# A routed feed-forward kernel: gathers four units ahead, the last units alone on TensorE, and an opening that turns two small inputs first

## The chip, the cores and the metric

The kernel runs on one core of a Trainium2 chip. The metric is the device time of one execution in microseconds. A core has five engines with instruction streams of their own: TensorE (PE: matrix products and transpositions), VectorE (DVE), ScalarE (ACT), GpSimd (POOL) and SyncE (SP, which here only issues transfers). They wait for each other through semaphores. Each of them takes its instructions in order, so that one that waits holds up all behind it.

## The reference

Two sequences of 2048 rows of 128 channels go through one layer:

```
mod = silu(c) @ wmod                                  # six rows of 128 for each sequence: sa ca ga sb cb gb
h = layernorm(x) * (1 + ca) + sa
x = x + ga * (mean of h over all rows up to this one) # softmax of a causal mask of zeros
h = layernorm(x) * (1 + cb) + sb
scores = softmax(h @ gate.T)                          # 8 experts
the 8192 largest of all 4096 * 8 scores are kept      # gate = score where kept, else 0
out = sum over experts of gate * (gelu(h @ W1 + b1) @ W2 + b2)  +  shared feed-forward of h
x = x + gb * out
```

## The kernel before

**The opening.** The 4096 rows are eight batches of 512. For each batch, DVE takes statistics (`stats1`), POOL makes the scale and bias of the normalisation (`rstd1`), ACT and DVE normalise into `XN` (`norm1`), PE transposes (`turn_x`), DVE forms the running means by a scan (`prefix`, with `INV` = 1 - 1/(t+1) made on ACT by `ratio(q)`), PE adds the transposed-back means to x in PSUM (`add_x`, `add_means`, with the diagonals `DCA`), and DVE adds a constant row `CBR` and keeps x (`keep_x2`). Then follow the second statistics (`stats2`) and normalisation, the logits and the rows written to a scratch tensor in memory. What the two sequences' vectors need comes from `modulation`: silu(c) on ACT, six products with `WMOD` on PE, and a chain of small instructions on DVE. Small vectors (biases, c, gate weights, 1/(t+1)) are loaded as rows of a tile `ROWS` in seven transfers from ACT's queue and transposed together into `COL`.

**The choice.** Thirty steps of a binary search on DVE and PE find the 8192nd score, between the products of the shared feed-forward on PE. Then lists of chosen rows are made (`IDXB`).

**The units.** The chosen pairs are sorted by expert and cut into units of 512 rows; a branch skips units that aren't used (up to 23; this input uses 18, numbered 0 to 17). For a unit v:

- POOL gathers its rows by four indirect transfers (`gather(v, s)`), 128 rows each, into one of ten places of `XG`;
- PE transposes them (`xt(v)`) and ACT copies them to `XT` (`copy_x(v)`);
- PE multiplies with W1 in four steps (`up`), ACT applies gelu to each, PE multiplies with W2 in four steps (`down`), ACT adds the bias (`ye(v)`, tile `YE`);
- PE transposes back (`yt(v)`), DVE multiplies with the scores (`yo(v)`, tile `YO`), which waits until the scatter of unit v - 2 has landed;
- POOL scatters with addition (`scatter(v)`, four indirect transfers), which waits until the scatter of unit v - 1 has landed.

POOL's order is 36 gathers, then for each unit its scatter and behind it a gap in which `gathered(v) - gathered(v - 1)` further gathers are issued. PE, ACT and DVE go through steps `s`, each with a unit v and a part c, four to a unit. `down` follows `up` by `LAG` = 2 steps, so that a unit's last two `down` lie in the next unit's steps. At c = 2 of unit v, PE does `yt(v - 1)` and then `xt(v + 1)`.

The lines of the view names: L920 is a gather, L933 a scatter, L956 a transposition by TensorE, L1067 `up` of a unit, L1093 `down`, L414 gelu, L430 `copy_x`, L439 `ye`, L799 the products of `yo`, L331 `ratio`, L395 `CBR`, L521 `keep_x2`, L997 `add_means`, L978 the products with `WMOD`, L974 the transposition of `ROWS`.

Of the kernel before, what the change touches and what calls it, by code (L numbers as in the profile page):

```python
# [15 lines left out]
P = 128  # L16
# [30 lines left out]
NSTEP = UNIT1 + NC * (NU + 3)  # L47
# [15 lines left out]
def gathered(v):  # L63

    return min(max(NT * AHEAD + PER_GAP * (v + 1), NT * (v + 5)), NT * NU)
# [18 lines left out]

def on_step(s):

    if 0 <= s < GS0:
        return s
    if UNIT1 <= s < UNIT1 + NC * NU:
        return s - UNIT1 + GS0  # L90
    return None


def adaln_moe(nc, x, gw, w1, b1, w2, b2, ws1, bs1, ws2, bs2, c_in, wmod, consts, ucon, icon, inv, out):
    rows_dram = nc.dram_tensor("rows_scratch", [S + NPAD, ROW], F32, kind="Internal").ap()

    with ExitStack() as ctx:
# [135 lines left out]
        def sync(eng):  # L233
# [25 lines left out]
            for b in range(2, NB):  # L259
                load_x(b)  # L260
            for q in range(1, NT):
                eng.dma_start(INV[:, q, :],
                              inv[0, q * BLK:(q + 1) * BLK].partition_broadcast(P)).then_inc(M["ld_inv"], 16)
# [21 lines left out]
            for s in range(NSTEP):  # L285
# [11 lines left out]
                v, c = (s - UNIT1) // NC, (s - UNIT1) % NC  # L297
# [971 lines left out]
```

## Time and profile before

| | us |
|---|---|
| median of 3 runs | 350.27 (349.93 to 351.46) |
| profiled execution, its own time | 349.06 |
| span of that execution | 347.3 |
| PE busy | 274.7 (79%) |
| POOL busy | 213.7 (62%) |
| DVE busy | 152.7 (44%) |
| ACT busy | 139.4 (40%) |

The span is from the first to the last instruction of the profiled execution; its time has some 1.8 us around it. Busy shares are averages over stages with different limits. The start times in the timeline are from the span's start. In a row of the timeline, the square bracket is the idle time before the instruction and what ended it.

### The profile page before, as it was taken

To read this page: it belongs to the slowest core of one execution; us is meant where nothing else is said; L and a number is where in the kernel's file an instruction comes from. 1 tells how busy PE (TensorE), PEld (TensorE's weight loads), DVE (VectorE), ACT (ScalarE), POOL (GpSimd) and SP (SyncE) were. 2 spreads that over 40 slices of the span, in tenths; PEclk is the share of its full clock that TensorE was granted. 3 is DMA by queue.
4 is the path that set the end of the run, shared out by engine and by line. 5 is a ranking of instruction groups with operands and counts; after the bars stand their busy time and mean duration, and the time that the engine had idled before them with its cause. 6 is when DMAs were issued, how large, how long until landed. Compare 5 with 4: busy or idle time off the path is not lost.

```text
span 347.3 us, 4624 instructions
## 1 busy us (share of the span) xinstructions
PE 274.7 (79%) x1044; PEld 141.8 (41%) x1044; DVE 152.7 (44%) x765; ACT 139.4 (40%) x236; POOL 213.7 (62%) x240
## 2 busy tenths in 40 slices
PE   5889985999989999999989899899595697495000
PEld 1757754343445554443444444444243243232000
DVE  2899773567677777344454544422101202102000
ACT  1669874354434434334334434344232333241000
POOL 4657540000027777677888888888787888765670
PEclk9999986899999999999999999999988989988555
DMA  7928420121025976655555665565535634333330
GB/s 205 307 70 227 108 63 0 30 64 15 0 75 143 282 226 174 176 96 84 116 115 114 106 109 114 116 120 119 114 41 127 142 46 68 75 28 33 33 29 1
DMA packets 49774, 35.70 MB, mean 103 GB/s; under 512 B 7816, under 2 KB 44495, under 8 KB 49744
## 3 DMA queue, kind: packets, MB, share of 16 engines
q0 software_dynamic: 13824, 14.46, 25.0%
q1 hardware_dynamic: 35794, 20.86, 21.6%
q8 instruction: 11, 0.18, 0.2%
q14 instruction: 19, 0.16, 0.1%
q10 hardware_dynamic: 126, 0.04, 0.0%
HBM read 23.40 MB, written 11.94 MB: 102 GB/s over the span
## 4 chain that ended last, share of the span: by engine, by line
PE 36%; POOL 17%; issue 14%; DVE 12%; DMA 8%; ACT 4%; SPq 3%; DVEq 1%; POOLq 0%; ACTq 0%
POOL out_dram L933 14%; PE Y L1093 12%; PE U L1061 9%; PE U L1067 5%; DMA out_dram<-YO,IDXB 4%; DVE GJ L750 4%; POOL R L920 3%; PE R1b L956 3%; DMA rows_scratch<-HT 2%; DVE YO L799 2%; PE R L1162 2%; ACT YE L439 2%; SPq L236 2%; DVE HM L724 2%; DMA INV<-in_inv_dram 1%
## 5 line engine op out<-in xcount | busy, mean ns | idle before, releaser
L933 POOL DMA_INDIRECT out_dram<-YO,IDXB x72 | 113.4, 1575 | 30.8 <-issue 19.8
L920 POOL DMA_INDIRECT R<-rows_scratch,IDXB x72 | 70.1, 973 | 72.1 <-DVE IDXB L765 50.5
L414 ACT ACTIVATE HF<-U,CB 128x512 f32<-128x512 f32 x72 | 49.5, 687 | 75.4 <-PE U L1067 74.4
L1067 PE MATMUL U<-XT,XW 128*128 128x512 f32 x144 | 77.3, 620 | 0.7 <-issue 0.7
L1093 PE MATMUL Y<-HF,XW 128*128 128x512 f32 x144 | 74.6, 602 | 0.0
L799 DVE SCALAR_TENSOR_TENSOR YO<-R1b,GT,R 128x128 f32<-128x128 f32 x72 | 20.3, 344 | 92.9 <-PE R1b L956 80.5
L1093 PEld LDWEIGHTS Y<-HF,XW 128*128 128x128 f32 x144 | 27.6, 198 | 31.4 <-issue 31.4
L1067 PEld LDWEIGHTS U<-XT,XW 128*128 128x128 f32 x144 | 26.7, 198 | 25.8 <-issue 25.5
L1061 PE MATMUL U<-H2F,WS 128*128 128x512 f32 x64 | 36.4, 655 | 0.0
L414 ACT ACTIVATE HF<-U,COL 128x512 f32<-128x512 f32 x32 | 21.9, 687 | 34.6 <-PE U L1061 34.5
L1093 PE MATMUL Y<-HF,WS 128*128 128x512 f32 x64 | 34.6, 623 | 0.0
L430 ACT ACTIVATE XT<-R 128x512 f32<-128x512 f32 x18 | 10.7, 597 | 40.4 <-PE R L956 40.4
L956 PE MATMUL R<-CST,R 128*128 128x128 f32 x76 | 13.5, 307 | 15.6 <-DMA R<-rows_scratch,IDXB 15.6
L750 DVE TENSOR_SCALAR_CACHE_REDUCE GJ<-R,UC 128x128 f32<-128x128 f32 x54 | 18.8, 349 | 1.2
L956 PE MATMUL R1b<-CST,YE 128*128 128x128 f32 x72 | 11.8, 287 | 9.2 <-ACT YE L439 9.2
L775 DVE COPY CB<-COL 128x4 f32 x18 | 4.6, 255 | 32.3 <-ACT HF L414 30.5
L956 PEld LDWEIGHTS R1b<-CST,YE 128*128 128x128 f32 x72 | 7.6, 141 | 24.1 <-ACT YE L439 24.1
L956 PEld LDWEIGHTS R<-CST,R 128*128 128x128 f32 x76 | 9.9, 157 | 17.3 <-DMA R<-rows_scratch,IDXB 16.7
L614 DVE TENSOR_SCALAR_CACHE_REDUCE TK<-SCT,TI 128x256 f32<-128x256 f32 x30 | 14.4, 479 | 1.1
L1093 PEld LDWEIGHTS Y<-HF,WS 128*128 128x128 f32 x64 | 11.0, 194 | 8.9 <-issue 8.8
L1162 PEld LDWEIGHTS R<-DQ,HM 128*128 128x128 f16 x108 | 6.9, 97 | 17.3 <-DVE HM L724 15.2
L439 ACT ACTIVATE YE<-Y,CB 128x512 f32<-128x512 f32 x18 | 12.2, 680 | 1.9 <-PE Y L1093 1.9
(172 smaller groups left out, 337.8 us busy)
## 6 DMA issues: line engine op xcount, KB each, us to landing
XW<-in_L_ffn_W_dram SPq DMA_DIRECT2D x36, 256.0 KB, 3.3
XW<-in_L_attn_x_dram SPq DMA_DIRECT2D x8, 256.0 KB, 6.3
rows_scratch<-GBC SPq DMA_DIRECT2D x2, 1024.0 KB, 8.1
rows_scratch<-HT SPq DMA_DIRECT2D x8, 256.0 KB, 2.5
out_dram<-SHO SPq DMA_DIRECT2D x8, 256.0 KB, 3.0
R<-rows_scratch,IDXB POOLq DMA_INDIRECT x72, 2.9
out_dram<-YO,IDXB POOLq DMA_INDIRECT x72
INV<-in_inv_dram SPq DMA_DIRECT2D x3, 256.0 KB, 4.3
```

The source lines that it names most:

```text
L414: eng.activation(HF[:, g % RING, :], UB[g % 2][:, :], ACT.Gelu_apprx_tanh, bias=bias).then_inc(M["a_gelu"], 1)
L439: eng.activation(YE[:, v % 2, :], YB[u % 2][:, :], ACT.Identity, bias=CB2[:, v % 3, :]).then_inc(M["a_ye"], 1)
L614: eng.tensor_scalar(GT, SCT[:, :], C_I.bitcast(F32), None, ALU.is_ge, ALU.add, accum_out=CNT[:, i % 2 * 2:i % 2 * 2 + 1]).then_inc(M["v_cn ...
L750: n = step("v_ix", eng.tensor_scalar(GJ[:, :], at, SIG[:, i:i + 1], None, ALU.is_le, ALU.add, accum_out=c0[:, s:s + 1]))
L799: m = eng.scalar_tensor_tensor(YO[:, k, t, :], RB[1][:, t * P:(t + 1) * P], GT4[:, k, t:t + 1], XG[:, r, t, D + E:ROW], ALU.mult, ALU.mult)
L920: eng.indirect_dma_start(XG[:, v % XR, s, :], None, rows_dram, bass.IndirectOffsetOnAxis(ap=IDXB[:, v, s:s + 1], axis=0)).then_inc(M[f"ld_ ...
L933: eng.indirect_dma_start(out, bass.IndirectOffsetOnAxis(ap=IDXB[:, v, s:s + 1], axis=0), YO[:, v % 2, s, :], None, compute_op=ALU.add).the ...
L956: m = eng.transpose(bank[:, t * P:(t + 1) * P], src(t), IDENT)
L1061: eng.matmul(bank[:, :], WS[:, c * P:(c + 1) * P], H2F[:, u * BLK:(u + 1) * BLK], start=True, stop=True).then_inc(M["pe_up"], 1)
L1067: eng.matmul(bank[:, :], WU[:, v % WR, c * P:(c + 1) * P], XT[:, v % 2, :], start=True, stop=True).then_inc(M["pe_up"], 1)
L1093: eng.matmul(bank[:, :], down_weights(g), HF[:, g % RING, :], start=c == 0, stop=c == NC - 1).then_inc(M["pe_dn"], 1)
L1162: m = eng.matmul(o, HM[:, v % 2, ch, s * P:(s + 1) * P], DQ[:, ch, :], start=ch == 0, stop=ch == 1)
```

## The change

It has three parts in one kernel.

- **Gathers**: the guaranteed lead of the gathers over the scatters falls from five units to four. The 36 gathers ahead of the first scatter and the two per gap stay.
- **Order of the last units**: from unit 12 on, a unit has six steps instead of four (`unit_step`), with `up` in the first four and `down` in the last four. `yt(v)` and then `xt(v + 1)` come in the last of them. So a unit is finished before the next one's rows are transposed.
- **Opening**: c and 1/(t+1) go into a small tile `FROWS` by two transfers of their own, are transposed ahead of `add_x(0)` and copied to `FCOL`. `ratio(0)` goes ahead of Silu on ACT. The other small vectors are transposed later, behind `add_x(1)`, and copied by `columns` behind `stats2(0)`. `WMOD` is loaded ahead of batch 1, the second part of `INV` ahead of batch 3 with a semaphore of its own. `CBR` is made and copied ahead of `norm1(2)`.

```
-    return min(max(NT * AHEAD + PER_GAP * (v + 1), NT * (v + 5)), NT * NU)
+    return min(max(NT * AHEAD + PER_GAP * (v + 1), NT * (v + 4)), NT * NU)
...
+ALONE = UMIN - 3
+LONG1 = UNIT1 + NC * (ALONE - 1)
+NSTEP = LONG1 + (NC + LAG) * (NU - ALONE + 1)
...
+def unit_step(s):
+
+    if s < LONG1:
+        return (s - UNIT1) // NC, (s - UNIT1) % NC
+    return ALONE - 1 + (s - LONG1) // (NC + LAG), (s - LONG1) % (NC + LAG)
...
 def on_step(s):
...
+    v, c = unit_step(s)
+    return GS0 + NC * v + c if c < NC and v < NU else None
...
-                    if c == 2:
-                        if 0 <= v - 1 < NU:
-                            yt(v - 1)
+                    if c == 2 and 0 < v < ALONE:
+                        yt(v - 1)
+                    if c == 2 and v + 1 < ALONE:
+                        xt(v + 1)
+                    if c == NC + LAG - 1:
+                        yt(v)
                         if v + 1 < NU:
                             xt(v + 1)
```

(ACT has the same with `ye` and `copy_x`; DVE does `yo(v)` in the last step.) The opening:

```
             load_x(0)
             eng.dma_start(CST[:, :], consts).then_inc(M["ld_cst"], 16)
+            eng.dma_start(WMOD[:, :], wmod).then_inc(M["ld_wmod"], 16)
             load_x(1)
-            eng.dma_start(WMOD[:, :], wmod).then_inc(M["ld_wmod"], 16)
...
+            load_x(2)
+            load_inv(1)
+            for b in range(3, NB):
...
+            eng.dma_start(FROWS[0:2, :], c_in).then_inc(M["ld_few"], 16)
+            eng.dma_start(FROWS[2:2 + SEQ // P, :], inv.rearrange("a (k p) -> (a k) p", p=P)).then_inc(M["ld_few"], 16)
...
-            eng.wait_ge(M["v_cols"], 1)
-            eng.activation(SIL, COL[:, 45:47], ACT.Silu).then_inc(M["a_sil"], 1)
...
+            ratio(0)
+            eng.wait_ge(M["v_few"], 1)
+            eng.activation(SIL, FCOL[:, 0:2], ACT.Silu).then_inc(M["a_sil"], 1)
             norm1(0)
-            ratio(0)
...
                 if j == 0:
+                    ratio(1)
                     diagonals()
-                    ratio(1)
-                    norm1(2)
                     eng.wait_ge(M["pe_cbr"], 1)
                     eng.activation(CBR[:, :, :].rearrange("p n c -> p (n c)"), RB[1][:, 0:2 * P],
                                    ACT.Copy).then_inc(M["a_cbr"], 1)
+                    norm1(2)
...
+            def columns():
+                eng.wait_ge(M["pe_cols"], 1)
+                eng.tensor_copy(COL[:, :], LG[:, 0:53]).then_inc(M["v_cols"], 1)
+                eng.wait_ge(M["v_cols"], 1)
                 eng.tensor_scalar(GBS, GG[:, 1, :], B2[:, 8:9], None, ALU.mult).then_inc(M["v_mod"], 1)
...
+                if j == 0:
+                    eng.wait_ge(M["ld_rows"], 80)
+                    eng.transpose(LG[:, 0:53], ROWS[0:53, :], IDENT[0:53, 0:53]).then_inc(M["pe_cols"], 1)
```

POOL before, from the scatter of unit 10 to that of unit 12 (a row with x3 is three transfers more of the same kind; `R` is the memory in which `XG` lies):

```order
L933 DMA out_dram<-YO,IDXB 4608x128 [waits s_st_sc1,s_v_yo]
L933 DMA out_dram<-YO,IDXB 4608x128 x3
L920 DMA R<-rows_scratch,IDXB 128x264 [waits s_pe_xt,s_v_yo,s_v_idx]
L920 DMA R<-rows_scratch,IDXB 128x264 x3
L933 DMA out_dram<-YO,IDXB 4608x128 [waits s_st_sc0,s_v_yo]
L933 DMA out_dram<-YO,IDXB 4608x128 x3
L920 DMA R<-rows_scratch,IDXB 128x264 [waits s_pe_xt,s_v_yo,s_v_idx]
L920 DMA R<-rows_scratch,IDXB 128x264 x3
```

The same place now:

```order
L968 DMA out_dram<-YO,IDXB 4608x128 [waits s_st_sc1,s_v_yo]
L968 DMA out_dram<-YO,IDXB 4608x128 x3
L955 DMA R<-rows_scratch,IDXB 128x264 [waits s_pe_xt,s_v_yo,s_v_idx]
L955 DMA R<-rows_scratch,IDXB 128x264
L968 DMA out_dram<-YO,IDXB 4608x128 [waits s_st_sc0,s_v_yo]
L968 DMA out_dram<-YO,IDXB 4608x128 x3
L955 DMA R<-rows_scratch,IDXB 128x264 x2
L968 DMA out_dram<-YO,IDXB 4608x128 [waits s_st_sc1,s_v_yo]
```

Each of these two gaps has two gathers instead of four; the four that are missing stand in the gap behind the scatter of unit 14.

PE before, where unit 11's output is transposed back (`R1b<-CST,YE`) and unit 13's rows are transposed (`R<-CST,R`) among the products of unit 12:

```order
L956 MATMUL R1b<-CST,YE 128x128 [waits s_v_yo,s_a_ye]
L956 MATMUL R1b<-CST,YE 128x128 x3
L1176 UNCONDITIONAL_BRANCH
L224 COMPARE_AND_BRANCH
L956 MATMUL R<-CST,R 128x128 [waits s_a_xh,s_ld_xg8]
L956 MATMUL R<-CST,R 128x128 x3
L1167 UNCONDITIONAL_BRANCH
L224 COMPARE_AND_BRANCH
L1067 MATMUL U<-XT,XW 128x512 [waits s_ld_wu1,s_a_xh,s_a_gelu]
```

And now a later unit's end and the next one's beginning:

```order
L1131 MATMUL Y<-HF,XW 128x512 [waits s_ld_wu1,s_a_gelu]
L1252 UNCONDITIONAL_BRANCH
L237 COMPARE_AND_BRANCH
L991 MATMUL R1b<-CST,YE 128x128 [waits s_v_yo,s_a_ye]
L991 MATMUL R1b<-CST,YE 128x128 x3
L1214 UNCONDITIONAL_BRANCH
L237 COMPARE_AND_BRANCH
L991 MATMUL R<-CST,R 128x128 [waits s_a_xh,s_ld_xg8]
L991 MATMUL R<-CST,R 128x128 x3
L1205 UNCONDITIONAL_BRANCH
L237 COMPARE_AND_BRANCH
L1105 MATMUL U<-XT,XW 128x512 [waits s_ld_wu2,s_a_xh,s_a_gelu]
```

The wait for gathered rows (`s_ld_xg8`) stood ahead of the older unit's products; it now stands behind its last `down` and its transposition back.

ACT before, at the opening (`SM<-COL` is the Silu, `R<-XW,RS` is `norm1`):

```order
L311 ACT_TABLE_LOAD
L311 ACTIVATE SM<-COL 128x2 [waits s_v_cols]
L321 ACTIVATE R<-XW,RS 128x128 [waits s_ld_x0,s_g_rs1]
L321 ACTIVATE R<-XW,RS 128x128 x2
L331 ACTIVATE INV<-R,CST 128x512 [waits s_ld_cst,s_pe_inv]
```

And now:

```order
L350 ACT_TABLE_LOAD [waits s_ld_cst]
L350 ACTIVATE INV<-R,CST 128x512 [waits s_pe_inv]
L388 ACT_TABLE_LOAD
L388 ACTIVATE SM<-FCOL 128x2 [waits s_v_few]
L338 ACTIVATE R<-XW,RS 128x128 [waits s_ld_x0,s_g_rs1]
```

`ratio(0)` moved ahead of the Silu, and a second load of ACT's table stands between them.

## Rows read from the trace of the kernel before

**Rows 1.** The page's costliest groups: the scatters, busy us and mean ns, idle before.

```profile
L933 POOL DMA_INDIRECT out_dram<-YO,IDXB x72 | 113.4, 1575 | 30.8 <-issue 19.8
```

**Rows 2.** Timeline of POOL, 148 to 331 us: start, length, instruction, idle before.

```profile
148.18 1.63 POOL L933 DMA_INDIRECT out_dram<-YO,IDXB  x1 [1.41 <-DVE YO L799]
...
209.56 1.62 POOL L933 DMA_INDIRECT out_dram<-YO,IDXB  x1 [0.30 <-issue]
...
219.72 1.62 POOL L933 DMA_INDIRECT out_dram<-YO,IDXB  x1 [0.30 <-issue]
...
250.84 1.62 POOL L933 DMA_INDIRECT out_dram<-YO,IDXB  x1 [0.99 <-DMA out_dram<-YO,IDXB]
...
262.21 0.95 POOL L920 DMA_INDIRECT R<-rows_scratch,IDXB  x1 [0.30 <-issue]
263.46 1.62 POOL L933 DMA_INDIRECT out_dram<-YO,IDXB  x1 [0.30 <-issue]
...
301.37 1.62 POOL L933 DMA_INDIRECT out_dram<-YO,IDXB  x1 [0.30 <-issue]
...
311.05 1.55 POOL L933 DMA_INDIRECT out_dram<-YO,IDXB  x1 [2.46 <-DMA out_dram<-YO,IDXB]
...
330.36 1.55 POOL L933 DMA_INDIRECT out_dram<-YO,IDXB  x1 [2.50 <-DMA out_dram<-YO,IDXB]
```

**Rows 3.** Timeline of PE, 265 to 291 us, transpositions and products of the units.

```profile
265.02 1.11 PE L956 MATMUL R<-CST,R 128*128 128x128 f32 x4 [3.28 <-DMA R<-rows_scratch,IDXB]
265.93 1.91 PE L1067 MATMUL U<-XT,XW 128*128 128x512 f32 x2
...
268.76 1.02 PE L1067 MATMUL U<-XT,XW 128*128 128x512 f32 x2
269.62 1.02 PE L1093 MATMUL Y<-HF,XW 128*128 128x512 f32 x2
...
290.25 0.66 PE L956 MATMUL R<-CST,R 128*128 128x128 f32 x4 [1.52 <-DMA R<-rows_scratch,IDXB]
```

**Rows 4.** Timeline, 290 to 300 us, ACT and DVE, one unit's work.

```profile
290.94 0.60 ACT L430 ACTIVATE XT<-R 128x512 f32<-128x512 f32 x1 [2.93 <-PE R L956]
...
297.54 0.68 ACT L439 ACTIVATE YE<-Y,CB 128x512 f32<-128x512 f32 x1
...
299.02 1.13 DVE L799 SCALAR_TENSOR_TENSOR YO<-R1b,GT,R 128x128 f32<-128x128 f32 x4 [4.96 <-PE R1b L956]
```

**Rows 5.** Timeline of the opening, all engines, 3 to 22 us.

```profile
3.41 1.28 ACT L311 ACT_TABLE_LOAD   x1 [3.41 <-issue]
...
4.69 2.07 PE L965 MATMUL Y<-XW,CST 128*128 128x512 f32 x2 [0.34 <-DMA CST<-in_consts_dram]
...
7.64 0.38 PE L974 MATMUL U<-CST,ROWS 71*128 71x71 f32 x1 [0.88 <-DMA ROWS<-in_inv_dram]
8.06 0.23 DVE L579 COPY COL<-U 128x71 f32<-128x71 f32 x1 [2.75 <-PE U L974]
...
8.58 2.72 PE L978 MATMUL U<-SM,WMOD 128*128 128x2 f32 x12 [0.56 <-ACT SM L311]
...
15.10 1.92 PE L997 MATMUL Y<-DCA,R 128*128 128x128 f32 x8
...
15.81 0.72 ACT L331 ACTIVATE INV<-INV,CST 128x512 f32<-128x512 f32 x1 [1.48 <-DMA INV<-in_inv_dram]
...
17.59 0.36 ACT L395 ACTIVATE CBR<-R1b 128x256 f32<-128x256 f32 x1
...
18.05 0.69 DVE L521 TENSOR_TENSOR X<-Y,CBR 128x512 f32<-128x512 f32 x1
...
18.52 0.84 PE L956 MATMUL U<-CST,R 128*128 128x128 f32 x4
...
21.15 0.66 DVE L521 TENSOR_TENSOR X<-Y,CBR 128x512 f32<-128x512 f32 x1
```

**Rows 6.** Transfers: KB each, median us from issue to landing.

```profile
WMOD<-in_L_wmod_dram SPq DMA_DIRECT2D x1, 384.0 KB, 5.8
```

**Rows 7.** Busy time and granted clock of TensorE in one microsecond.

```profile
core 0: us, PE busy (x) PEld busy (x) DVE busy (x) ACT busy (x) POOL busy (x), PEclk, DMA share, GB/s
60.00:61.00 1.00, 1.00 (x2) 0.47 (x3) 0.69 (x4) 0.00 (x0) 0.00 (x0) 0.50 0.00 0
```

More of the change, by code:

```diff
@@ L256, in sync, with load_inv @@
             eng.dma_start(CST[:, :], consts).then_inc(M["ld_cst"], 16)
+            eng.dma_start(WMOD[:, :], wmod).then_inc(M["ld_wmod"], 16)
             load_x(1)
-            eng.dma_start(WMOD[:, :], wmod).then_inc(M["ld_wmod"], 16)
-            for b in range(2, NB):
+            def load_inv(q):
+                eng.dma_start(INV[:, q, :], inv[0, q * BLK:(q + 1) * BLK].partition_broadcast(P)).then_inc(
+                    M["ld_inv1" if q == 1 else "ld_inv"], 16)
+            load_x(2)
+            load_inv(1)
+            for b in range(3, NB):
                 load_x(b)
-            for q in range(1, NT):
-                eng.dma_start(INV[:, q, :],
-                              inv[0, q * BLK:(q + 1) * BLK].partition_broadcast(P)).then_inc(M["ld_inv"], 16)
+            load_inv(2)
+            load_inv(3)
             eng.dma_start(UC[:, :], ucon).then_inc(M["ld_uc"], 16)
@@ L334, in diagonals @@
             def diagonals():
-                eng.wait_ge(M["v_mod"], 9)
-                for d, c, n in ((DCA, CA, 0), (DCB, CB, 0), (DCB, CB, 1), (DCA, CA, 1)):
+                eng.wait_ge(M["v_mod"], 8)
+                for d, c, n in ((DCB, CB, 0), (DCB, CB, 1), (DCA, CA, 0), (DCA, CA, 1)):
                     eng.activation(d[:, n, :], IDENT, ACT.Identity, scale=c[:, n:n + 1]).then_inc(M["a_dg"], 1)
@@ L577, in vector @@
             stats1(0)
-            eng.wait_ge(M["pe_cols"], 1)
-            eng.tensor_copy(COL[:, :], UB[0][:, 0:55 + SEQ // P]).then_inc(M["v_cols"], 1)
+            eng.wait_ge(M["pe_few"], 1)
+            eng.tensor_copy(FCOL[:, :], RB[2][:, 0:2 + SEQ // P]).then_inc(M["v_few"], 1)
+            norm1(0)
             stats1(1)
-            norm1(0)
             stats1(2)
@@ L591, in vector @@
                     stats2(j - 1)
+                if j == 1:
+                    columns()
                 if j + 3 < NB:
@@ L970, in tensor @@
             eng.wait_ge(M["ld_cst"], 16)
+            eng.wait_ge(M["ld_few"], 32)
+            nf = 2 + SEQ // P
+            eng.transpose(RB[2][:, 0:nf], FROWS[:, :], IDENT[0:nf, 0:nf]).then_inc(M["pe_few"], 1)
             add_x(0)
-            nr = 55 + SEQ // P
-            eng.wait_ge(M["ld_rows"], 112)
-            eng.transpose(UB[0][:, 0:nr], ROWS[0:nr, :], IDENT[0:nr, 0:nr]).then_inc(M["pe_cols"], 1)
             eng.wait_ge(M["a_sil"], 1)
@@ L1215, in tensor @@
                             down(g)
-                    if c == 2:
-                        if 0 <= v - 1 < NU:
-                            yt(v - 1)
+                    if c == 2 and 0 < v < ALONE:
+                        yt(v - 1)
+                    if c == 2 and v + 1 < ALONE:
+                        xt(v + 1)
+                    if c == NC + LAG - 1:
+                        yt(v)
                         if v + 1 < NU:
```

61 lines of the change are left out of this document (33 added, 28 removed).

## The prediction

> **What bounds the kernel now.** I read the page first: GpSimd's scatters are the costliest group of the kernel, and the idle time in front of them is mostly "issue", not a wait for another engine [rows 1]. Then the timeline of POOL alone. Scatter 0 starts at 148.18 after a wait of 1.41 us for YO of unit 0, the last time that POOL waits for an engine's work. From there its row is full: a unit with two gathers in its gap costs 219.72 - 209.56 = 10.16 us; with four gathers (301.37 - 263.46) / 3 = 12.64 us; with none 311.05 - 301.37 = 9.68 us, of which 2.46 are the wait for the scatter before to land [rows 2]. So from 148 us on the end is set by how many such gaps there are, and TensorE matters only if a unit's YO comes late.
>
> Two things follow. First, everything up to 148.18 shifts the end one for one, because the gathers of that stage end 1.41 us before YO(0) is there: both chains start from the same opening. Second, a landing wait of 2.46 us is bare in a gap without gathers and covered in a gap with two or four of them.
>
> **The gathers.** Before, the gaps after scatters 9 to 17 hold 2, 4, 4, 4, 4, 0, 0, 0, 0 gathers. After, they hold 2, 2, 2, 4, 4, 4, 0, 0, 0: the number is the same (36 ahead and 36 in gaps), but gap 14, bare before, is now filled. From scatter 10 to scatter 17, before: 4 x 12.64 + 3 x 9.68 = 79.6 (the trace: 330.36 - 250.84 = 79.5). After: 2 x 10.16 + 3 x 12.64 + 2 x 9.68 = 77.6. That is **-2.0 us**: one landing wait of 2.46 is covered, and each two-gather gap keeps 0.3 to 0.5 of its own issue time. Bound from the other side: the gap after scatter 9 has two gathers and still waited 0.99 where others show 0.30 [rows 2]. If both new two-gather gaps did that, 1.4 us would come back, leaving -0.6. That extra wait fell where unit 11's Y was done and its weight buffer's refill started; in the new gaps TensorE is idle for gathers by then, so I take none of it.
>
> **Does TensorE keep up?** Gathers for unit 17 now run after scatter 14. Scatter 10 stays at 250.84, so by the sum above scatter 14 starts at 296.4, 15 at 309.1, 16 at 318.8 and 17 at 328.4. The last gather of unit 17 starts 11.4 us after scatter 14 (262.21 - 250.84), at 307.8, and a transpose of gathered rows starts 265.02 - 262.21 = 2.8 us after the last gather's start [rows 2, 3]: 310.6.
> The time of a unit alone, by rows: four transposes 0.66, copy 0.60, eight up/down products (each 1.02, but 0.86 from one start to the next) 7.0, YE 0.68, four transposes back 0.66, with some 0.2 us of hand-over: 9.8 us. YO's four products add 1.13 [rows 3, 4]. After a pause of 3.28 us for gathers the transposes took 1.11 in place of 0.66 and the next product 1.91 in place of 1.02; 3.7 us after the restart the products are at 1.02 again [rows 3]. That costs a unit about 1.5 us. So YO(17) is ready at 310.6 + 9.8 + 1.1 + 1.5 = 323.0, 5.4 us before scatter 17 wants it. Units 14, 15, 16 by the same sum are ready at 285, 298 and 310 for scatters at 296, 309 and 319. Unit 13's output no longer waits for unit 14's gathers, which is what the new PE order gives; with the old order YO(16) would stand behind the transposes of unit 17 at 310.6, and come about 3 us late for its scatter. The PE edit is hidden by POOL at a cost of nothing; without that cover it would cost the 1.6 us by which 9.8 + 1.5 exceeds POOL's 9.68, in each of the last units.
>
> **The opening.** c and 1/(t+1) come in two transfers of their own and are transposed as soon as the constants are there. Before, the transposition stood until 7.64 for the last of seven loads; the constants had landed at 4.68 [rows 5]. But ACT is now ahead with ratio(0), whose first table load waits for the constants, and the order of the changed kernel shows a second load before Silu, where there was one. A load took 1.28 [rows 5]. So: 4.68 + 1.28, INV 0.7, 1.28 again, Silu 0.2: the products with WMOD can start at 8.2 in place of 8.58, a gain of 0.4, not of the 2.5 that the earlier transposition suggests. WMOD took 5.8 us to land [rows 6]; it is now issued some 0.5 earlier and ahead of x1, so it is there. x1 goes behind 384 KB and should land near where WMOD did, about 8.4, and be used then; x1's later statistics take back about 0.2 of the 0.4.
> CBR is copied right after the diagonals. Before, ratio(1) waited 1.48 for INV, norm1(2) stood behind it, and CBR came at 17.59 to 17.95; keep_x2(0) started at 18.05 although the means were done at 15.10 + 1.92 = 17.02 [rows 5]. After, the means set it, at about 17.2: -0.85.
> Then the moved part comes: on PE the transposition of 53 columns (0.38) stands in front of turn_x(2), which began at 18.52 [rows 5]; on DVE a copy like the one of 0.23 and a small product stand between stats2(0) and stats1(4), up to 0.45 together. PE's add_x(1) ends near 18.95, the columns at 19.15, the means of batch 1 near 20.85, and keep_x2(1) starts at 20.85 in place of 21.15. From there DVE is busy without a gap for four batches, so what holds at keep_x2(1) holds later: **-0.3 us**. Bounds: the whole 18.05 - 17.02 = 1.0 with the 0.4 kept, and 0.2 of the column work hidden: -1.2. None of the gains and 0.38 + 0.45 of new work: +0.8.
>
> **A rule against it.** The table load's row lasts 1.28 us and I take that for its whole cost [rows 5]. The Trainium skill, "ScalarE: Activation LUTs", section "What ACT_TABLE_LOAD costs", puts a switch to another set at 1.28 us plus a drain of about 1.38, so 2.66. By that, the two loads would make the Silu 2.8 us later than I have it. My sum does without it.
>
> **Sum.** -2.0 - 0.3 = -2.3 us on the profiled execution, whose time was 349.06 with a span of 347.3 (347.3 - 330.36 = 16.9 us of span come after scatter 17's start and stay): 346.8. The median of the runs is 350.27, 1.2 above the profiled execution; from it, 350.27 - 2.3 = **348.0 us**. I give the time against the median. The three runs lie 1.5 us apart, and 0.5% (1.75 us) is about what a measurement of this kernel can tell from no change.
>
> **The rivals.**
> 1. *The opening gives more* (x1 comes early and the column work is hidden): -1.2 there, 347.1. For it: the means are done 1.0 us before keep_x2(0) uses them. Chance 0.13.
> 2. *The opening gives nothing or loses*: +0.1 to +0.8, so 348.4 to 349.1. For it: the column work lies exactly where PE and DVE are both full. To this belongs chance in the clock: between 60 and 61 us the granted clock is 0.50 with PE busy for 1.00 of 1.00 us [rows 7]; where such a stretch begins may move with the opening by a microsecond in either direction. Chance 0.18.
> 3. *The change doesn't do what it says in the tail*: the two-gather gaps show the landing (0.99 in place of 0.30) and gap 14's saving is spent: 350.27 - 0.3 - 0.6 = 349.4. For it: the gap after scatter 9. Against: the other gaps of that kind. Chance 0.09.
> 4. *A load costs more than its row*: ACT works through two loads, each with a drain behind it as long again as the row, and the Silu comes at 10.9. DVE and PE have no slack behind the modulation, so 2.4 us of the delay against 8.58 stay, less the 0.85 that CBR gives: +1.5, with the tail 349.8. It is what the Trainium skill's section on ACT_TABLE_LOAD, named above, would make of it. The row at 3.41 neither shows nor excludes a drain. Chance 0.04.
> 5. *Slower: TensorE becomes the bound of the tail.* A unit alone has pauses for the copy, the gelu and YE, and the granted clock may not come back in them. Unit 14's transposes start 8.8 us after scatter 11 (10.16 less a gather) and 2.8 behind, at 261.0 + 8.8 + 2.8 = 272.6. If units of u microseconds then follow one another without a pause, YO(17) is there at 272.6 + 4u + 1.1. It decides from u = 13.7, where that passes 328.4; from u = 14.6 the kernel is slower than before by over 0.5%. With the eight products at half speed throughout u is 9.8 + 7 = 16.8, YO(17) comes at 340.9, and scatter 17 10.6 us later than before: 350.27 - 0.3 + 10.6 = 360.6. Against: the clock came back within 3.7 us in a unit of the same products [rows 3]. Chance 0.05.
> The forecast, 346.9 to 348.6 with its centre at 348.0, has 0.51.
>
> **How the numbers follow.** Faster by over 0.5% means under 348.5: nearly all of the forecast (0.49), rival 1 (0.13), some of rival 2 (0.04): 0.66. Slower by over 0.5% means over 352.0: rival 5, 0.05. The rest, 0.29, is within 0.5%. The range takes in the forecast, rivals 1 to 3 and the run-to-run spread: 346.3 to 349.8.
>
> **What would show it.** In the profile after: POOL's scatters 10 to 17 at steps of 10.2, 10.2, 12.6, 12.6, 12.6, 9.7, 9.7; the last four-gather block behind scatter 14; the waits of 2.5 us twice, not three times. On PE, the transposes of YE before those of the next unit's rows, and YO of units 14 to 17 waiting for DMA or for nobody. In the opening: two table loads, Silu near 8.0, keep_x2(0) near 17.2 and keep_x2(1) near 20.9. I am wrong if scatter 0 starts later than 148.2, if a scatter of unit 12 or later waits for YO, or if two-gather gaps cost over 10.6.

## The result, and the profile after

| | us |
|---|---|
| before, median of 6 runs beside the changed kernel | 350.25 (348.75 to 351.46) |
| changed, median of 6 runs | 346.58 (345.72 to 347.69) |
| ratio, with its 95% interval | 0.990 (0.987 to 0.993) |
| profiled execution of the changed kernel, its own time and span | 346.52 and 344.7 |

The changed kernel is 3.7 us faster by the medians; the interval makes that 2.5 to 4.6 us. The profiled executions differ by 2.5 us (349.06 and 346.52). Here and below, an execution over 1.5% above the fastest of its kernel counts as slow: the ratios, unlike the medians, leave such ones out, and they are not the quotients of the medians; the traces of e6 and e9 are of slow ones. The page has the scatters' group as before, with 2.4 us less idle time in front of them than in [rows 1]:

```profile
L968 POOL DMA_INDIRECT out_dram<-YO,IDXB x72 | 113.6, 1577 | 28.4 <-issue 21.0
```

The timeline of POOL, with the rows that answer to [rows 2]: the first transfers of scatters 0 and 10 to 17.

```profile
147.97 1.63 POOL L968 DMA_INDIRECT out_dram<-YO,IDXB  x1 [1.68 <-DVE YO L832]
...
250.37 1.62 POOL L968 DMA_INDIRECT out_dram<-YO,IDXB  x1 [0.62 <-issue]
...
260.52 1.65 POOL L968 DMA_INDIRECT out_dram<-YO,IDXB  x1 [0.30 <-issue]
...
270.67 1.62 POOL L968 DMA_INDIRECT out_dram<-YO,IDXB  x1 [0.30 <-issue]
...
283.33 1.62 POOL L968 DMA_INDIRECT out_dram<-YO,IDXB  x1 [0.30 <-issue]
...
295.97 1.62 POOL L968 DMA_INDIRECT out_dram<-YO,IDXB  x1 [0.30 <-issue]
...
308.62 1.62 POOL L968 DMA_INDIRECT out_dram<-YO,IDXB  x1 [0.30 <-issue]
...
318.22 1.55 POOL L968 DMA_INDIRECT out_dram<-YO,IDXB  x1 [2.38 <-DMA out_dram<-YO,IDXB]
...
327.77 1.55 POOL L968 DMA_INDIRECT out_dram<-YO,IDXB  x1 [2.42 <-DMA out_dram<-YO,IDXB]
```

Steps of 10.15, 10.15, 12.66, 12.64, 12.65, 9.60 and 9.55 us: two gathers, two, four, four, four, none, none. A wait of 2.4 us for a landing stands twice where it stood three times. From scatter 10 to scatter 17 the trace has 77.40 us, before 79.52: -2.12. Up to scatter 10 it has -0.47. That isn't the opening's gain: at scatter 0 it is -0.21 (148.18 and 147.97), at scatter 9 only -0.07 (239.99 and 239.92), and the rest is the idle time ahead of scatter 10, 0.62 in place of 0.99. So the tail's gain is in this pair of traces whole, and the opening's nearly gone by scatter 0.

TensorE in the last units, to be read against [rows 3]: `R<-CST,R` is the transposition of a unit's rows, `R1b<-CST,YE` that of its output.

```profile
297.52 0.66 PE L991 MATMUL R<-CST,R 128*128 128x128 f32 x4 [2.54 <-DMA R<-rows_scratch,IDXB]
298.91 1.15 PE L1105 MATMUL U<-XT,XW 128*128 128x512 f32 x1 [0.73 <-issue]
...
308.49 0.66 PE L991 MATMUL R1b<-CST,YE 128*128 128x128 f32 x4 [0.78 <-ACT YE L462]
...
310.14 0.66 PE L991 MATMUL R<-CST,R 128*128 128x128 f32 x4 [0.99 <-DMA R<-rows_scratch,IDXB]
311.53 0.67 PE L1105 MATMUL U<-XT,XW 128*128 128x512 f32 x1 [0.73 <-issue]
...
319.60 0.66 PE L991 MATMUL R1b<-CST,YE 128*128 128x128 f32 x4 [0.78 <-ACT YE L462]
```

Unit 16 (297.52) and unit 17 (310.14) wait for their gathers, and each is finished before the next one's rows are turned. The six `up` records after a pause take 4.51 us in unit 16, where the clock had fallen (0.50 from 299 to 302 us), and 3.00 in unit 17, where it stood at 1.00. YO of units 14 to 17 starts at 284.93, 295.07, 309.24 and 320.35 for scatters at 295.97, 308.62, 318.22 and 327.77.

The opening, all engines, against [rows 5]:

```profile
4.86 1.28 ACT L350 ACT_TABLE_LOAD   x1 [4.86 <-DMA CST<-in_consts_dram]
...
6.16 0.69 ACT L350 ACTIVATE INV<-R,CST 128x512 f32<-128x512 f32 x1
6.86 1.28 ACT L388 ACT_TABLE_LOAD   x1
...
8.16 0.20 ACT L388 ACTIVATE SM<-FCOL 128x2 f32<-128x2 f32 x1
...
8.41 0.80 PE L1013 MATMUL U<-SM,WMOD 128*128 128x2 f32 x3 [1.28 <-ACT SM L388]
...
11.51 0.88 ACT L338 ACTIVATE R<-XW,RS 128x128 f32<-128x128 f32 x2 [2.00 <-POOL RS L903]
12.68 0.71 ACT L350 ACTIVATE INV<-INV,CST 128x512 f32<-128x512 f32 x1
...
16.99 0.69 DVE L547 TENSOR_TENSOR X<-Y,CBR 128x512 f32<-128x512 f32 x1 [0.48 <-PE Y L1030]
...
18.98 0.21 DVE L581 COPY COL<-LG 128x53 f32<-128x53 f32 x1
...
19.36 0.67 DVE L508 BATCH_NORM_STATS2 ST<-XW 128x6 f32<-128x128 f32 x3
...
20.56 0.66 DVE L547 TENSOR_TENSOR X<-Y,CBR 128x512 f32<-128x512 f32 x1
```

INV's second part is used at 12.68 without a wait (before 15.81, after 1.48 of waiting), and the first `keep_x2` comes at 16.99 (18.05), the second at 20.56 (21.15).

### The profile page after: what moved, and what is told of

It is laid out like the page before. It is cut to its first block, busy times and chain, and to the rows that moved or that the text cites. A ratio compares the mean times of both kernels' runs of the same rounds, so it can differ in the third digit from the quotient of the medians.

```text
span 344.7 us, 4630 instructions
## 1 busy us (share of the span) xinstructions
PE 275.6 (80%) x1045; PEld 140.6 (41%) x1045; DVE 151.6 (44%) x766; ACT 141.2 (41%) x237; POOL 213.9 (62%) x240
## 4 chain that ended last, share of the span: by engine, by line
POOL 44%; issue 22%; PE 17%; DMA 7%; DVE 3%; ACT 3%; POOLq 1%; SPq 0%; ACTq 0%; DVEq 0%
POOL out_dram L968 29%; POOL R L955 15%; PE U L1099 6%; PE Y L1131 5%; DMA out_dram<-YO,IDXB 3%; DMA rows_scratch<-HT 3%; DMA XW<-in_L_attn_x_dram 2%; PE Y L1030 1%; PE R L1051 1%; PE R L991 1%; DVE ST L508 1%; ACT H2F L372 1%; PE LG L1051 1%; ACT R L338 1%; PE R1b L991 1%
## 5 line engine op out<-in xcount | busy, mean ns | idle before, releaser
L1131 PE MATMUL Y<-HF,XW 128*128 128x512 f32 x144 | 72.1, 596 | 0.0
L1131 PEld LDWEIGHTS Y<-HF,XW 128*128 128x128 f32 x144 | 26.5, 190 | 29.4 <-issue 29.4
L991 PE MATMUL R<-CST,R 128*128 128x128 f32 x76 | 12.5, 290 | 13.6 <-DMA R<-rows_scratch,IDXB 13.6
L462 ACT ACTIVATE YE<-Y,CB 128x512 f32<-128x512 f32 x18 | 12.3, 682 | 11.3 <-PE Y L1131 11.3
L1200 PE MATMUL R<-DQ,HM 128*128 128x129 f16 x108 | 9.3, 221 | 4.3 <-DVE HM L757 4.3
```

Source lines behind the costliest of these rows:

```text
L462: eng.activation(YE[:, v % 2, :], YB[u % 2][:, :], ACT.Identity, bias=CB2[:, v % 3, :]).then_inc(M["a_ye"], 1)
L991: m = eng.transpose(bank[:, t * P:(t + 1) * P], src(t), IDENT)
L1131: eng.matmul(bank[:, :], down_weights(g), HF[:, g % RING, :], start=c == 0, stop=c == NC - 1).then_inc(M["pe_dn"], 1)
L1200: m = eng.matmul(o, HM[:, v % 2, ch, s * P:(s + 1) * P], DQ[:, ch, :], start=ch == 0, stop=ch == 1)
```

## The experiments

All were timed beside runs of the kernel before on the same chip. Three jobs ran on three chips. On the second and third, every kernel, that of before too, took 360 to 370 us: between 105 and 160 us ScalarE and VectorE stood still some 4 to 5 us about every 14 us (in the version with the new order alone, VectorE's row at 111.09 has "3.92 <-remote" in front of it), so that scatter 0 came at 162 to 168 us in place of 148. What held them there I did not find out. Steps ahead of 105 us and the intervals of the tail read as on the first chip; the ratios are less sharp there. The runs on the second and third chip are e5 to e8 and e9 to e12.

### The two halves, and the control (e1, e2, e3)

e1 is the kernel before with the tail's edits, e2 with the opening's:

```
e1:  -    ... NT * (v + 5)), NT * NU)
     +    ... NT * (v + 4)), NT * NU)      and unit_step, ALONE, the new order on PE, ACT, DVE
e2:  +    FROWS, FCOL, columns(), ratio(0) ahead of Silu, the new order of transfers, CBR ahead of norm1(2)
e3:       the changed kernel itself
```

> The gathers' lead and the order of the last units alone, with the opening of before. By the sum of the prediction the end moves by one covered landing wait less the issue of two-gather gaps: scatter 10 to scatter 17 takes 77.4 us (79.5 before), the time falls by 2.0 to 2.4 us, ratio 0.994. Rival, that the measured 3.7 us between the medians come from the tail: 3.1 us or more, ratio 0.991. Rival, that the opening carries it: the time falls by under 1.5.

> The opening alone, with five units' lead and the old order of the units. keep_x2(1) starts at 20.6 in place of 21.15 and scatter 0 between 147.2 and 148.0. By the trace of the changed kernel 0.2 to 0.6 us are left at the end, ratio 0.998 to 0.999. Rival, that the profiled execution understates the opening, since the granted clock comes back at another time in each execution: 1.0 to 1.5 us, ratio 0.996.

> The changed kernel again, beside its parts on the same chip. If the parts add up, its gain is that of the tail alone and of the opening alone together, 2.5 to 3.0 us. If it stays at 3.7 with parts of 2.1 and 0.5, the parts help each other, or one of the two medians was by chance.

| | median us (before: 349.61) | ratio | scatter 10 to 17, us |
|---|---|---|---|
| e1 tail alone | 347.57 | 0.9931 (0.9897 to 0.9964) | 77.56 |
| e2 opening alone | 348.69 | 0.9969 (0.994 to 0.9997) | 79.98 |
| e3 both | 347.55 | 0.9953 (0.9931 to 0.9975) | 77.40 |

The tail's edits carry their 2 us by themselves: 2.4 by the ratio, 2.0 by the medians. (The 79.98 of e2 has a last landing wait of 3.09, where the kernel before had 2.50.) The opening's edits are worth 1.1 us by e2's ratio, with an interval from 0.1 to 2.1, but e2's trace doesn't show that gain at the end. Its second `keep_x2` comes at 20.09 (before 21.15) and its scatter 0 at 149.10, where 147.2 to 148.0 had been expected; between the two the clock, below, took more than the opening gave. The trace of the control, e3, shows the same, with its first `keep_x2` at 16.36 and its scatter 0 later than the kernel before's 148.18:

```profile
148.70 1.63 POOL L968 DMA_INDIRECT out_dram<-YO,IDXB  x1 [1.66 <-DVE YO L832]
```

The control gained 1.6 us by the ratio (2.1 by the medians), not 3.7: its interval and the first one meet at 0.993 at most. It also missed its expectation of 2.5 to 3.0. The parts, 2.4 and 1.1, don't add up in this job: the control is no faster than the tail alone (347.55 and 347.57). So the tail's gain is shown, and the opening's is shown only as far as the `keep_x2`; at the end of the kernel it rests on e2's interval. With the third session (e9, 0.9929) the changed kernel has three ratios, 0.990, 0.9953 and 0.9929; their mean is 0.9927, 2.6 us.

### Gathers without the order, order without the gathers, and a lead of three (e5, e6, e7)

```
e5:  unit_step and ALONE taken out: four steps to every unit, yt(v - 1) and xt(v + 1) at c == 2
e6:  -    ... NT * (v + 4)), NT * NU)
     +    ... NT * (v + 5)), NT * NU)
e7:  -    ... NT * (v + 4)), NT * NU)
     +    ... NT * (v + 3)), NT * NU)
```

> The changed kernel with its opening and its gathers (lead of four units), but the old order of the last units on TensorE: four steps to a unit, the transposition of the next unit's rows at the third of them, and a unit's output transposed behind it. My theory: the gathers' -2.1 us needs the new order. Unit 17's gathers land at about 309.9 as in the changed kernel, but unit 16's last up, its downs and the transposition of its output stand behind the transposition of unit 17's rows: 310.1 + 0.7 + some 7 of products + 1.5 of low clock + YE 0.7 = 320, so YO(16) near 320.5. Scatter 16 starts at about 320.5 with an idle wait for YO instead of 318.2, scatter 17 near 330.1, scatter 10 to scatter 17 79.7 us instead of 77.4, and the kernel takes about 349.0 (ratio to before 0.997). Rival 1, GpSimd alone sets the tail: the interval stays at 77.4 and the time at that of the changed kernel (ratio 0.991 to 0.994). Rival 2, unit 15 is late as well and the delays add: 81.5 or more, ratio about 1.002.

> The changed kernel with its opening and the new order of the last units on TensorE, but the gathers five units ahead as before. My theory: the order by itself is worth nothing, since GpSimd's row is full: scatter 10 to scatter 17 takes 79.5 us with three landing waits of 2.5, and the kernel has the opening's gain alone, as the version with the opening alone (ratio 0.995 to 0.998). YO of units 14 to 17 comes ahead of its scatter by even more than in the changed kernel. Rival: the order moves TensorE's pauses or weight refills so that the gaps on GpSimd change by themselves; then the interval differs from 79.5 by over 0.3 us.

> The changed kernel with a guaranteed lead of three units instead of four: the gaps after scatters 10 to 17 hold 2, 2, 2, 2, 4, 4, 0, 0 gathers, one landing wait fewer than in the changed kernel. By GpSimd's row alone scatter 10 to scatter 17 would be 4 x 10.15 + 2 x 12.65 + 9.6 = 75.5 us, 1.9 less than 77.4. My theory: TensorE is now the limit. Unit 17's gathers stand behind scatter 15 at 303.7; the last starts at 315.0 and lands at 317.3, and from its transposition to its YO it takes the 10.2 us that the changed kernel's trace shows (310.14 to 320.35): YO at 327.5, scatter 17 at about 328.7 with an idle wait for YO. Interval 78.3, time 0.9 us above the changed kernel (ratio to before 0.994). Rival, GpSimd alone: interval 75.5, time 1.9 us below it (ratio 0.985).

| | median us (before: 365.56) | ratio | scatter 10 to 17, us |
|---|---|---|---|
| e5 gathers, old order | 369.38 | 1.0056 (0.9996 to 1.0117) | 81.29 |
| e6 order, old gathers | 366.20 | 0.9964 (0.9913 to 1.0015) | 79.39 |
| e7 lead of three | 370.33 | 1.0098 (1.0047 to 1.015) | 84.12 |

By the intervals of the tail, the order alone is worth nothing (79.39, before 79.52) and the gathers alone cost 1.8 us; together they give 2.1. POOL of e5, the first transfers of scatters 13, 15 and 16:

```profile
301.10 1.62 POOL L953 DMA_INDIRECT out_dram<-YO,IDXB  x1 [2.13 <-DVE YO L819]
...
328.31 1.62 POOL L953 DMA_INDIRECT out_dram<-YO,IDXB  x1 [2.21 <-DVE YO L819]
...
338.01 1.55 POOL L953 DMA_INDIRECT out_dram<-YO,IDXB  x1 [2.48 <-DVE YO L819]
```

Units 13 and 15 are late, by 1.9 us each (the steps to their scatters are 14.51 and 14.57 where four gathers take 12.65); unit 16's wait is no longer than that for a landing. So the sum is near rival 2 of that expectation, though the unit that I had named is not the one. The reason is on TensorE of e5, at unit 15:

```profile
315.20 0.90 PE L976 MATMUL R<-CST,R 128*128 128x128 f32 x3 [4.62 <-DMA R<-rows_scratch,IDXB]
316.11 1.06 PE L1090 MATMUL U<-XT,XW 128*128 128x512 f32 x1
...
319.52 1.06 PE L1090 MATMUL U<-XT,XW 128*128 128x512 f32 x1
...
326.15 0.66 PE L976 MATMUL R1b<-CST,YE 128*128 128x128 f32 x4 [0.50 <-ACT YE L452]
```

The transposition of unit 16's rows stops TensorE 4.62 us for gathers while unit 15's products are half done, the clock is low when it goes on, and unit 15's output is transposed only at 326.15. Unit 13 has the same, behind a pause of 8.84. With the old order, a pause for gathers is paid by the unit before. In e7 the same happens to the unit itself:

```profile
323.61 1.64 POOL L968 DMA_INDIRECT out_dram<-YO,IDXB  x1 [3.35 <-DVE YO L832]
...
351.45 1.55 POOL L968 DMA_INDIRECT out_dram<-YO,IDXB  x1 [7.91 <-DVE YO L832]
```

By GpSimd's row alone this interval would have been 75.5 us; it is 84.1. I had expected 78.3, with unit 17 alone late. In fact unit 15 was late too: its last gathers stand in the gap of two behind scatter 13, TensorE waited 7.59 us for them (transposition at 309.41), and the first six `up` took 5.13 at a low clock. That delay pushed unit 17's gathers back, and its scatter with them. The clock was low again behind unit 17's own pause of 5.59 us, so that it took 12.3 us from its transposition (337.78) to its YO (350.05), where I had put 10.2.

### The clock between the opening and the search (e4, e8, e12)

e4 and e12 have one edit on ScalarE, which leaves one table load where there were two; e8 has it and four products that nobody reads:

```
e4, e12:  +            eng.wait_ge(M["g_half"], 1)
          +            eng.activation(EXPT, NHALF[:, 0:1], ACT.Silu)
                       (ahead of ratio(0))
e8 also:       logits(NB - 1)
          +    for _ in range(4):
          +        eng.matmul(RB[1][:, :], ONES, H2F[:, 0:BLK], start=True, stop=True)
```

> The changed kernel with an activation of one column of Silu ahead of ratio(0), so that ACT needs one table load, while the constants are still on their way. Theory: Silu of c runs near 6.0 in place of 8.16, but the products with WMOD start only when WMOD has landed, near 8.0, and batch 1's normalisation (11.51) is set by x1 and POOL, so keep_x2(1) moves by less than 0.2 us and the time by 0 to 0.2. Rival, that the Silu is what the opening waits for: 0.5 us or more less than the changed kernel. By the Trainium skill's 2.66 us for a switch of sets 3 us would go; the trace of the changed kernel had 1.28 from the load's start to the activation.

> The changed kernel with a Silu of one column ahead of ratio(0) (one table load, as in the version run before) and, new here, four products of 128x512 into an unused bank of PSUM behind the last logits on TensorE, 3.4 us of work that nobody reads, in the 3.4 us between 53.6 and 57.0 in which TensorE was idle and after which the granted clock stood at 0.50 until about 61. Theory A, the idle time brings the low clock: it stays at 1.00 through 54 to 61 us, the first steps of the search take 1.0 us each instead of 1.9, and scatter 0 comes about 2 us earlier than 145.9: 144, ratio to before about 0.986. Theory B, what falls is set by something else (the time of the execution, or the search's small products): clock and time stay, ratio 0.991. Theory C: the products delay the first product of the search, +0.5.

> The changed kernel with a Silu of one column ahead of ratio(0), so that ScalarE loads one table instead of two, again, beside the control on the same chip. Theory A: the one load fewer brings the Silu of c from 8.2 to about 5.5 to 6.4 and the first keep_x2 0.3 to 0.4 us forward, and that is all that can be told from the order: 0.3 to 0.6 us less than the control. Theory B: where the half-clock stretches of TensorE fall decides over more than that: between 50 and 64 us the clock record differs from the control's, and the first step of the search moves by a microsecond or more, in either direction.

e4 took 346.36 us, ratio 0.9913 (0.9885 to 0.9942), the lowest median of its job; e12 362.32, ratio 0.9899 (0.9841 to 0.9956), beside a control of 363.78 and 0.9929 (0.9887 to 0.9971). The Silu of c came at 5.49 and 5.72 in place of 8.16, and yet the first `keep_x2` came at 16.65 and 17.14, no earlier than in e3 and e9 (16.36 and 16.70). That is as e4's theory has it, and not the 0.3 to 0.4 us forward that theory A of e12 had expected. The timeline of e12, ScalarE, shows why:

```profile
3.51 1.28 ACT L387 ACT_TABLE_LOAD   x1 [3.51 <-issue]
...
5.72 0.19 ACT L390 ACTIVATE SM<-FCOL 128x2 f32<-128x2 f32 x1
...
11.65 0.88 ACT L338 ACTIVATE R<-XW,RS 128x128 f32<-128x128 f32 x2 [2.86 <-POOL RS L905]
```

ScalarE then waits 2.86 us for `rstd1(1)`, the statistics of x1. In the changed kernel it waits 2.00 in the same place (11.51): the second load lies inside that wait, and x1's statistics set the opening.

So what made e4's trace short? The granted clock. The windows of 2 us of e4:

```profile
core 0: us, PE busy (x) PEld busy (x) DVE busy (x) ACT busy (x) POOL busy (x), PEclk, DMA share, GB/s
50.00:52.00 2.00, 1.57 (x12) 1.11 (x10) 1.17 (x9) 1.14 (x2) 0.05 (x1) 1.00 0.00 0
52.00:54.00 2.00, 1.64 (x15) 1.55 (x14) 0.28 (x2) 0.31 (x1) 0.00 (x0) 1.00 0.00 0
54.00:56.00 2.00, 0.00 (x0) 0.00 (x0) 1.53 (x7) 1.71 (x3) 0.00 (x0) 0.54 0.00 0
```

and of the changed kernel:

```profile
core 0: us, PE busy (x) PEld busy (x) DVE busy (x) ACT busy (x) POOL busy (x), PEclk, DMA share, GB/s
50.00:52.00 2.00, 2.00 (x6) 0.86 (x5) 1.61 (x11) 0.00 (x0) 0.50 (x3) 0.50 0.00 0
52.00:54.00 2.00, 1.93 (x12) 1.58 (x10) 0.00 (x0) 1.36 (x2) 0.00 (x0) 0.70 0.00 0
54.00:56.00 2.00, 1.40 (x13) 1.31 (x12) 0.51 (x2) 0.20 (x1) 0.00 (x0) 1.00 0.00 0
```

In e4 the clock stays at full speed from 50 to 54 us, where the changed kernel had 0.50 and 0.70. e3 and e9, which are the changed kernel too, had a low stretch there and one more at 23 to 26. From the first `keep_x2` to the first step of the search (VectorE's scan of TI) the time goes with the number and the length of such stretches in every trace with the same work:

| stretches below full clock between 12 us and the end of the logits | traces | us from the first keep_x2 to the first step |
|---|---|---|
| none | e4, e11 | 39.6, 39.7 |
| one, 48 to 54 | before, after, e1, e6, e7, e10, e12 | 40.8 to 41.3 |
| one longer, 48 to 55 | e5 | 42.5 |
| two, 23 to 26 and 50 to 54 | e2, e3, e9 | 43.0 |

A stretch costs 1.1 to 2.2 us by these rows, as much as either half of the change. e4 and e12 are one kernel, with 39.6 and 41.3, and e12's first step came 1.3 us ahead of its control's (58.44 and 59.71), which is its theory B. Ahead of the stretch at 23 to 26, TensorE had stood still 1.13 to 1.14 us (until 21.1 in e2, 20.8 in e3 and 21.2 in e9); in the other traces the pause there is 0.2 to 1.1. e4 has 1.06 and no stretch, so the pause goes with it but isn't shown to bring it.

e8 was to prevent the low stretch that follows the logits by keeping TensorE busy. It did not:

```profile
55.38 5.38 PE L1118 MATMUL R1b<-H2F,CST 128*128 128x512 f32 x8
```

```profile
core 0: us, PE busy (x) PEld busy (x) DVE busy (x) ACT busy (x) POOL busy (x), PEclk, DMA share, GB/s
54.00:56.00 2.00, 2.00 (x16) 1.76 (x16) 0.40 (x2) 0.19 (x1) 0.00 (x0) 1.00 0.00 0
56.00:58.00 2.00, 2.00 (x4) 0.76 (x3) 1.41 (x7) 1.82 (x3) 0.00 (x0) 0.55 0.00 0
58.00:60.00 2.00, 2.00 (x4) 0.86 (x3) 0.00 (x0) 1.01 (x2) 0.00 (x0) 0.60 0.00 0
```

TensorE was busy for all of 54 to 60 us, and the clock fell during the second of these rows: it is 0.59 from 56 to 57 us and 0.50 from 57 to 59. The four products (two records each) took 5.38 us, where four at the full clock take 3.4 (0.86 each, [rows 3]), and the search began at 60.80, in place of 56.26 in e4 and 58.44 in e12. VectorE stood 2.94 us in front of it for TensorE: theory C, but with far more than the 0.5 us expected. Its first steps then ran at the full clock, one in 1.0 us, where e4's third and fourth came 2.0 and 1.9 behind the one before. The ratio was 0.9962 (0.9914 to 1.001). So that stretch comes without idle time ahead of it too; theory A is false, and what brings the stretch stays open.

### Single terms of the opening (e9, e10, e11)

```
e10:       (j == 0)
      +                    norm1(2)
                           eng.wait_ge(M["pe_cbr"], 1)
                           eng.activation(CBR[...], RB[1][:, 0:2 * P], ACT.Copy).then_inc(M["a_cbr"], 1)
      -                    norm1(2)
e11:  +                    eng.transpose(LG[:, 0:53], ROWS[0:53, :], IDENT[0:53, 0:53])
      +                eng.tensor_copy(GJ[:, 0:53], LG[:, 0:53])
```

> The changed kernel itself, for the runs beside it on this chip. If this chip has no pauses of all engines at once between 105 and 160 us, about 346.6 to 347.6 and a ratio to before of 0.990 to 0.995; scatter 10 to scatter 17 77.4 us on any chip.

> The changed kernel, but with the normalisation of batch 2 back ahead of the copy of CBR on ScalarE. In the changed kernel CBR ends at 15.67 and the means at 16.96, which release the first keep_x2 at 16.99; so there are 1.3 us between. Theory A, the means set it and CBR's place is worth nothing, because what had held CBR before was the second part of INV, which now lands in time: CBR ends near 16.1, the first keep_x2 stays within 0.15 of 17.0, the time within 0.3 us of the changed kernel. Theory B, CBR's place is what brought the first keep_x2 forward by 1.06: it goes back towards 17.5 to 18.0 and the second by 0.3 or more.

> The changed kernel with the moved column work doubled: the transposition of the 53 columns is done twice on TensorE behind add_x(1), and VectorE copies them twice (the first copy into an unused place). Theory A, VectorE is the bound there and TensorE's part is hidden: the second keep_x2 comes 0.1 to 0.25 us later than in the control, by the one copy more of 0.21, and everything after by as much. Theory B, TensorE's part shows too: 0.5 us later. Theory C, both are hidden: no change.

e9 took 363.78 us, 0.9929 (0.9887 to 0.9971), scatter 10 to 17 77.77. Its chip had the pauses, so the times expected without them don't apply, and 0.15 of a wait came back at unit 12's scatter. e10 took 361.25, 0.9898 (0.9847 to 0.9949); e11 362.39, 0.9917 (0.9882 to 0.9953). The three can't be told apart by time, but their timelines decide. e10, ScalarE and VectorE:

```profile
12.74 0.71 ACT L350 ACTIVATE INV<-INV,CST 128x512 f32<-128x512 f32 x1
...
15.68 0.36 ACT L416 ACTIVATE CBR<-R1b 128x256 f32<-128x256 f32 x1
...
17.05 0.69 DVE L547 TENSOR_TENSOR X<-Y,CBR 128x512 f32<-128x512 f32 x1 [0.74 <-PE Y L1030]
```

With `CBR` back behind `norm1(2)` it is there at 16.04, and the first `keep_x2` at 17.05, the second at 20.58 (changed kernel 16.99 and 20.56). The control on the same chip, e9, has 16.70 and 20.18, but e10's rows show what held the first `keep_x2`: it waited 0.74 us for TensorE's means, 1.0 us after `CBR` was there. So `CBR`'s new place is worth nothing, theory A. What had held it before was, by the rows, INV's second part, which now lands in time; no version changed that alone. e11, VectorE, the two copies and the second `keep_x2`:

```profile
19.05 0.18 DVE L581 COPY GJ<-LG 128x53 f32<-128x53 f32 x1
19.14 0.20 DVE L582 COPY COL<-LG 128x53 f32<-128x53 f32 x1
...
20.72 0.66 DVE L547 TENSOR_TENSOR X<-Y,CBR 128x512 f32<-128x512 f32 x1
```

One copy more costs 0.09 us from one start to the next. From the first to the second `keep_x2` it is 3.60 us, against 3.57 in the changed kernel, 3.48 in e9 and 3.53 in e10: 0.03 to 0.12 more, about what such traces differ by. Theory B's 0.5 is out, so TensorE's second transposition is hidden; between theories A and C this doesn't decide.

## Why the prediction was right

The forecast was 348.0 us, and 346.58 was measured. That is inside the range but below the forecast's own 346.9 to 348.6; the mechanism is right in the tail, and in the opening the agreement is partly luck.

**The tail, -2.0.** Right, term by term: -2.12 in the trace. The gaps' prices were 10.16, 12.64 and 9.68 and came out at 10.15, 12.65 and 9.6. Scatters 14 to 17 were forecast at 296.4, 309.1, 318.8 and 328.4 and came at 295.97, 308.62, 318.22 and 327.77, each 0.4 to 0.6 early, which scatter 10 already was by 0.47. Rival 3 falls: neither new gap of two showed its landing. The gap after scatter 9 still did, with 0.62 in place of 0.99.

Two statements ahead of the sum are only partly borne out: that "everything up to 148.18 shifts the end one for one", and that a landing wait is covered in a gap with two gathers. Some gaps of two end with more than the 0.30 us of idle time that the others show. In the kernel before, scatter 1 waited 0.76 us for a landing, as scatter 10 did 0.99. In the other traces 0.6 to 2.1 us stand ahead of scatters 1, 2, 8, 9 or 10, mostly put down to the landing, and from scatter 0 to scatter 10 the traces take 102.4 to 105.1 us. e4 is 2.30 ahead of the kernel before at scatter 0 and 1.71 at scatter 10. So a gap of two gathers covers the landing wait in the two new gaps (within 0.2 us in every trace with a lead of four and the new order), but not everywhere.

**TensorE keeps up.** Right. The rows of unit 17 were turned at 310.14 (forecast 310.6) and YO(17) came at 320.35 (323.0). The forecast had 1.5 us too much for a low clock that did not come in that unit, and its YO's own 1.1, which lies behind the start; unit 17's rows were 0.5 earlier than forecast, and the unit alone took 0.4 longer (10.2 from transposition to YO, forecast 9.8). Rival 5, TensorE as the bound, is false at a lead of four and true at three (e7) and with the old order (e5). The prediction said that the order costs nothing and that without it YO(16) would be about 3 us late. e5 shows the direction, a loss of 3.9 us against the new order, but in units 13 and 15, not 16.

**The opening, -0.3.** The sign was right; the term was sized too small, and one step named the wrong edit. Measured: -1.06 at the first `keep_x2` (forecast -0.85), -0.59 at the second (-0.3), -0.61 at the last (46.62 to 46.01), and 1.1 us by e2. At scatter 0 only 0.21 was left of it, and in e3, the same kernel, scatter 0 came at 148.70. That is one of the prediction's own signs of being wrong ("if scatter 0 starts later than 148.2"). So "what holds at keep_x2(1) holds later" is true in the first trace up to the last `keep_x2` and fails behind it, where the clock's stretches lie; that 0.21 at scatter 0 is near the forecast's 0.3 is luck. The step "CBR is copied right after the diagonals ... After, the means set it" was right in its second half only: e10 shows that the copy's place does nothing, which by the rows leaves INV's earlier landing. The columns' work was put at up to 0.45 on VectorE and measured 0.38 (18.98 to 19.36).
The step on the Silu was right in time (forecast 8.0 to 8.2, measured 8.16; products 8.41, forecast 8.2) and beside the point: `norm1(1)` waits 2.00 us for the statistics of x1 behind it. Those start at 8.11 in place of 8.21 in the kernel before, and 7.79 in e3, where the first `keep_x2` is 0.63 earlier too. So x1's statistics took nothing back, where the prediction had put 0.2: they stand right behind batch 0's row on VectorE, without a wait for x1.

**The table load.** From the start of a load to the start of the activation behind it are 1.30 us both times (4.86 to 6.16, 6.86 to 8.16), and the second load begins where the activation before it ends (6.16 + 0.69). The 2.66 of the Trainium skill, "ScalarE: Activation LUTs", section "What ACT_TABLE_LOAD costs", is not seen in this trace: if a drain is there, it does not delay the next activation. Rival 4 falls. One load fewer (e4, e12) brings the Silu 2.4 to 2.7 us forward and the first `keep_x2` by nothing.

**The clock.** Rival 2 spoke of a stretch that could move the opening "by a microsecond in either direction". That is what stands between the term of the opening and the medians: 1.0 us gained at the first step of the search (59.01 to 58.01) was 0.5 by 64 us, where the clock came back at nearly the same time as before, and 0.21 at scatter 0; and the ratio moved between 0.990 and 0.9953 for one kernel. That the median of the first session (346.58) lies 1.4 us under the forecast is of this size, and I can't assign it further. Over three sessions the change is worth 2.6 us against the 2.3 of the forecast. Each session shows one trace of a kernel, but every execution has its mean granted clock on record. In the 35 of the kernel before beside e1 to e4, time and clock go together (correlation -0.74; 2.7 us less for 0.01 more clock). The changed kernel's six executions have 0.9255 on average and e3's twelve 0.9228, which by that slope is 0.7 us, an estimate, of the 1.0 between their medians. That the clock is the cause of that, and not a companion, is not shown.

No version tried is surely faster than the changed kernel. The one with a single table load had a ratio lower by 0.004 and 0.003 than its control in both jobs, with intervals that overlap. For e4 the timeline gives no reason but the clock, and e12's trace hasn't e4's short stage (41.3 and 39.6 us).

## What to carry to other kernels

- Where one engine's queue is full, count its units of work by kind and price each gap from the trace; the sum of the tail was 77.6 us and the trace has 77.40. A wait in such a queue is worth covering only as long as the engine that feeds it keeps its slack: here a lead of four gains 2.1 us and one of three loses 4.6.
- An engine that stops for a late input in the middle of older work delays that older work. Finish a unit before waiting for the next one's data, and change the order and the lead together: here either alone gained nothing.
- Before believing a difference of 1 us, look at the granted clock in windows, in more than one trace of the same kernel.

## What was not expected of the hardware

The granted clock of TensorE falls to 0.50 (1.2 of 2.4 GHz) for 3 to 7 us at one to three places in the first 66 us, and the same kernel has it at other places in another execution: at 23 to 26 us in e3 and e9 and not in the changed kernel's first trace, which has the same instructions. It fell in e8 after more than 2 us in which TensorE had been busy throughout. And of three chips, two paused ScalarE and VectorE for some 4 to 5 us about every 14 us while the lists of rows were made, and scatter 0 came 14 to 20 us later, with the same program and input.
